# Attention on all four 64x64 tiles of TensorE, with the mask added in four half-size operations

## The chip, the core and the metric

The kernel runs on one core of a Trainium2 chip. Its engines work side by side and meet at semaphores: TensorE (PE; weight loads are shown as PEld), VectorE (DVE), ScalarE (ACT), GpSimd (POOL) and SyncE (SP), which starts DMAs. The metric is the device time of one execution in microseconds; less is better.

TensorE's array of 128 x 128 cells can be addressed in quarters, tiles of 64 x 64. The row half is given by the partitions on which the two inputs lie in SBUF, the column half by the partitions of PSUM that the output goes to. A float32 matmul stands in the trace as two records, each with its own weight load.

## What is computed

The reference is a small tower over 32 sequences of 64 tokens with 1024 features: a diagonal state-space filter, a rotary attention with 16 heads, a dequantized linear layer, a Mamba block and a linear layer with routed low-rank experts, each added to the residual. The change is in the attention:

```
q, k = rotary(x @ Wq), rotary(x @ Wk);  v = x @ Wv        # 16 heads of 64
logits = einsum('bhqd,bhkd->bhqk', q, k)
logits = where(causal, logits, -1e9) / sqrt(64)
attn = softmax(logits)
out = einsum('bhqk,bhkd->bhqd', attn, v)
h = h + out @ Wo
```

All of it is in float32; large products are split into a high and a low part in a rounded float32 form.

## The kernel before

The tokens are worked through in 4 blocks of 8 sequences (NB = 8, S = 64, so T = 512 tokens per block). Each block goes through all layers before the next one starts. Each weight matrix comes as strips of 128 output features: DMA brings a strip (`raw`), ScalarE makes its high part (`wh`), GpSimd the rest (`wl`, line 537), and TensorE runs 24 matmuls over it (`strip`, line 985). The order of all work is written out by hand, one program per engine, with semaphores between them.

Attention takes the 16 heads in 8 pairs (KC = 8), the one head on partitions 0 to 63, the other on 64 to 127. Per pair j TensorE runs three strips (q, k, v), and between them, for the pair of the step before, the transposes of the probabilities (`turned`, line 1093) and the weighted products (`weighted`, line 1105); behind the three strips come `logits` (line 1120) and the transposes of v (`values`, line 1129), which wait for VectorE's scaling of v (semaphore s_vT, line 1735). VectorE does the rotary sums, adds the mask (line 1686), takes the softmax (lines 1689 to 1695) and copies the outcome out of PSUM (line 1716); ScalarE does the exponential and the copies of v (`vf`) and of the transposed probabilities (`pT`).

In `logits` there are 16 small matmuls, for each sequence bb one of either head e: the head sets the row half and the column half alike, and the PSUM bank 2 + e. So head 0 is always computed in the tile (row half 0, column half 0) and head 1 in (1, 1). After it, `sm` has a head on each half of its partitions, all queries of a sequence in 64 columns.

The 16 transposed probability tiles lie in `pT` with the even sequences on partitions 0 to 63 and the odd ones on 64 to 127, side by side in the columns for the two halves of `sm`. In `weighted`, before, the eight matmuls of the even sequences come first (row half 0, column half e), then the eight of the odd ones (row half 1), into the banks 2 and 3.

Of the kernel before, what the change touches and what calls it, by code (L numbers as in the profile page):

```python
# [18 lines left out]
ALU = mybir.AluOpType  # L19
# [3 lines left out]
P = 128  # L23
# [3 lines left out]
NB = 8  # L27
# [155 lines left out]
def tower(nc, ins, out, nblk=NBLK, stop=9):  # L183
    with ExitStack() as ctx:
# [743 lines left out]
        def _(pe):  # L928
# [155 lines left out]
            for b in range(nblk):  # L1084
                if stop >= 2:
# [11 lines left out]
                    def weighted(j):  # L1097

                        pe.wait_ge(s_ptc, b * KC + j)
                        settle(pe)  # L1100
                        for par in range(2):
                            for bb in range(par, NB, 2):
                                for e in range(2):
                                    r0 = 64 * par
                                    ins_ = mm(psx[64 * e:64 * e + 64, 2 + par, bb * S:(bb + 1) * S],
                                              vf[r0:r0 + 64, (bb // 2) * P + 64 * e:(bb // 2) * P + 64 * e + 64],
                                              pT[r0:r0 + 64, (bb // 2) * P + 64 * e:(bb // 2) * P + 64 * e + 64],
                                              start=True, stop=True)
                        ins_.then_inc(s_pv, 1)

                    def logits(j):

                        pe.wait_ge(s_rot, b * 16 + 2 * j + 2)
                        if j >= 1:
                            pe.wait_ge(s_ao, b * KC + j)
                        settle(pe)
                        for bb in range(NB):
                            for e in range(2):
                                r0 = 64 * e
                                ins_ = mm(psx[r0:r0 + 64, 2 + e, bb * S:(bb + 1) * S],  # L1120
                                          qc[r0:r0 + 64, bb * S:(bb + 1) * S], kc[r0:r0 + 64, bb * S:(bb + 1) * S],
                                          start=True, stop=True)
                        ins_.then_inc(s_logit, 1)
# [301 lines left out]
        def _(v):  # L1425
# [249 lines left out]
            for b in range(nblk):  # L1675
                if stop >= 2:
                    norm(b, 0)
                    for j in range(KC + 1):
                        if j >= 1:
                            own = Own(v, s_own["soft"], b * 4 * KC + 4 * (j - 1))  # L1680
                            v.wait_ge(s_logit, b * KC + j)
                            if j >= 2:
                                v.wait_ge(s_ptm, b * KC + j - 1)
                            for e in range(2):
                                r = slice(64 * e, 64 * e + 64)
                                ins_ = tt(sm[r, :, :], psx[r, 2 + e, :].rearrange("p (b s) -> p b s", b=NB),
                                          over_b("causal", 64 * e, 64 * e + 64), ALU.add)
                            own.link(ins_)
                            own.link(v.tensor_reduce(smx[:, 0, :], sm[:, :, :], AXX, ALU.max))
                            tt(sm[:, :, :], sm[:, :, :], smx[:, 0, :].unsqueeze(2).to_broadcast([P, NB, S]),  # L1690
                               ALU.subtract).then_inc(s_ein, 1)
                            v.wait_ge(s_exp, b * KC + j)
                            own.link(v.tensor_reduce(smx[:, 1, :], sm[:, :, :], AXX, ALU.add))
                            own.link(v.reciprocal(smx[:, 1, :], smx[:, 1, :]))
                            tt(sm[:, :, :], sm[:, :, :], smx[:, 1, :].unsqueeze(2).to_broadcast([P, NB, S]),
                               ALU.mult).then_inc(s_prob, 1)
# [284 lines left out]
```

## Time and profile before

| | us |
|---|---|
| median of 3 runs | 4029.22 |
| lowest, highest | 4028.99, 4029.43 |
| profiled execution | 4035.27 |
| its span, first to last instruction | 4033.5 |
| TensorE matmuls busy | 3869.3 (96%) |
| VectorE busy | 2690.4 (67%) |
| GpSimd busy | 2212.4 (55%) |
| ScalarE busy | 2057.1 (51%) |
| granted clock of TensorE, mean | 0.984 of full |

The profile is one execution. Busy time is the time in which at least one instruction of the engine was under way; since matmuls overlap in the array, many records can be in flight at once, and their ends are modelled. "x" with a number is a count of records. Weight loads (PEld) overlap the matmuls. An arrow in brackets behind a row gives the idle time of the engine just before it, and who ended it; "issue" stands for no releaser that the profile shows.

### The profile page before, as it was taken

What the parts mean: (1) busy time and instruction counts of PE and PEld (TensorE: products, weight loads), DVE (VectorE), ACT (ScalarE), POOL (GpSimd) and SP (SyncE); (2) the same over time, 40 slices, a digit from 0 to 9 for tenths busy, and PEclk for the clock granted to TensorE, in tenths of its full rate; (3) what the DMA queues carried; (4) which work ended last, traced back from release to release, by engine and by line L of the source; (5) the groups of instructions that cost most, each with busy time, mean ns of one, the idle gap of its engine ahead of it and who ended that gap; (6) DMA issues with size and microseconds to landing.
All of it is one profiled execution on the core that took longest, in us unless ns stands there. A gap on an engine that the chain in (4) does not pass through costs nothing.

```text
span 4033.5 us, 59248 instructions
## 1 busy us (share of the span) xinstructions
PE 3869.3 (96%) x22816; PEld 2547.3 (63%) x22816; DVE 2690.4 (67%) x2934; ACT 2057.1 (51%) x3012; POOL 2212.4 (55%) x960
## 2 busy tenths in 40 slices
PE   4899999999999999999999999999999999999999
PEld 1568777444777777544577877744477877744466
DVE  6855572999446573699835555499935557289953
ACT  7842344777332344777523233677723234387732
POOL 0023433999534343799733334599943343389962
PEclk7999999999999999999999999999999999999999
DMA  4242234000322224200132223400032223410022
GB/s 114 79 145 80 86 104 159 23 16 16 118 93 86 79 84 137 98 16 16 61 114 95 79 77 117 153 13 16 26 125 94 84 84 105 160 31 16 16 89 73
DMA packets 97131, 320.23 MB, mean 79 GB/s; under 512 B 12400, under 2 KB 16752, under 8 KB 92400
## 3 DMA queue, kind: packets, MB, share of 16 engines
q1 hardware_dynamic: 80752, 275.70, 21.4%
q10 hardware_dynamic: 16128, 41.03, 3.0%
q8 instruction: 176, 2.88, 0.3%
q14 instruction: 75, 0.61, 0.1%
HBM read 272.51 MB, written 44.17 MB: 79 GB/s over the span
## 4 chain that ended last, share of the span: by engine, by line
PE 36%; issue 32%; DVE 20%; POOL 9%; ACT 2%; POOLq 0%; ACTq 0%; DVEq 0%
PE psg L985 22%; DVE sb_wst L1798 17%; POOL sb_wl L537 9%; PE psx L1220 5%; PE psg L1241 3%; PE psx L1293 1%; PE psg L1271 1%; DVE psg L1771 1%; DVE psg L1770 1%; PE psg L1369 1%; PE psg L1278 1%; ACT sb_yh L898 1%; PE psx L1002 0%; PE psg L1260 0%; PE psg L1195 0%
## 5 line engine op out<-in xcount | busy, mean ns | idle before, releaser
L537 POOL TENSOR_TENSOR sb_wl<-sb_raw,sb_wh 128x1024 fp32r<-128x1024 f32 x388 | 955.1, 2465 | 1740.9 <-ACT sb_wh L654 1740.6
L1798 DVE TENSOR_TENSOR_SCAN sb_wst<-sb_dA,psx 128x1024 f32<-128x1024 f32 x512 | 1130.0, 2268 | 12.3 <-PE psx L1220 10.4
L654 ACT ACTIVATE sb_wh<-sb_raw 128x1024 fp32r<-128x1024 f32 x388 | 407.4, 1053 | 544.1 <-PE psg L985 268.8
L796 ACT ACTIVATE sb_dA<-sb_dlt,sb_a_sb 128x504 f32<-128x504 f32 x1024 | 647.3, 705 | 56.0 <-DVE sb_wst L1798 53.8
L1220 PEld LDWEIGHTS psx<-sb_dgB,sb_duT 64*128 64x128 f32 x4096 | 359.9, 188 | 447.5 <-DVE sb_wst L1798 309.1
L1220 PE MATMUL psx<-sb_dgB,sb_duT 64*128 64x256 f32 x4096 | 587.5, 406 | 35.3 <-DVE sb_wst L1798 33.3
L1241 PE MATMUL psg<-sb_wst,sb_cst 64*64 64x512 f32 x4096 | 605.7, 617 | 0.9 <-ACT sb_twin L787 0.9
L572 POOL TENSOR_TENSOR sb_wst<-sb_wst,sb_cb_lo 128x1024 f32<-128x1024 f32 x256 | 600.3, 2370 | 5.0 <-DVE sb_wst L1798 5.0
L572 POOL TENSOR_TENSOR sb_wst<-sb_wst,sb_cb_hi 128x1024 f32<-128x1024 f32 x248 | 577.6, 2365 | 24.7 <-DVE sb_wst L1798 24.7
L985 PE MATMUL psg<-sb_xh,sb_wh 128*128 128x512 f32 x2080 | 535.6, 400 | 16.1 <-POOL sb_wl L537 7.1
L985 PE MATMUL psg<-sb_xh,sb_wl 128*128 128x512 f32 x2080 | 516.7, 390 | 0.0
L985 PE MATMUL psg<-sb_xl,sb_wh 128*128 128x512 f32 x2080 | 513.9, 389 | 0.0
L985 PEld LDWEIGHTS psg<-sb_xh,sb_wh 128*128 128x128 f32 x2080 | 384.0, 189 | 112.8 <-issue 15.3
L985 PEld LDWEIGHTS psg<-sb_xh,sb_wl 128*128 128x128 f32 x2080 | 391.2, 188 | 83.2
L985 PEld LDWEIGHTS psg<-sb_xl,sb_wh 128*128 128x128 f32 x2080 | 390.4, 188 | 81.3
L1241 PEld LDWEIGHTS psg<-sb_wst,sb_cst 64*64 64x64 f32 x4096 | 123.3, 132 | 186.2 <-issue 186.1
L1824 DVE TENSOR_TENSOR psg<-psg,sb_rstd 128x512 f32<-128x512 f32 x60 | 42.0, 699 | 286.0 <-PE psg L985 286.0
L1876 DVE TENSOR_TENSOR sb_h<-sb_h,psg 128x512 f32<-128x512 f32 x32 | 22.0, 687 | 257.1 <-PE psg L985 222.9
L1760 DVE SCALAR_TENSOR_TENSOR sb_cv<-psg,sb_conv,sb_cv 128x504 f32<-128x504 f32 (+2 forms) x192 | 141.0, 734 | 27.8 <-DVE sb_cv L1758 4.1
L787 ACT ACTIVATE sb_twin<-psg 128x512 f32<-128x512 f32 x128 | 69.3, 593 | 118.6 <-PE psg L1249 118.6
L705 ACT ACTIVATE sb_ah<-sb_ao 128x512 fp32r<-128x512 f32 x32 | 20.2, 632 | 193.2 <-DVE sb_ao L1716 193.2
L662 ACT ACTIVATE sb_xh<-sb_xc 128x512 fp32r<-128x512 f32 x128 | 79.2, 618 | 76.6 <-DVE sb_xc L1599 66.6
(278 smaller groups left out, 4946.9 us busy)
## 6 DMA issues: line engine op xcount, KB each, us to landing
sb_raw<-in_w SPq DMA_DIRECT2D x360, 512.0 KB, 3.6
sb_raw<-w_ffn_dequantized SPq DMA_DIRECT2D x32, 512.0 KB, 3.3
gates<-sb_gt ACTq DMA_DIRECT2D x64, 256.0 KB, 2.6
sb_gin<-gates SPq DMA_DIRECT2D x64, 256.0 KB, 2.6
h_after_tok<-sb_h SPq DMA_DIRECT2D x4, 2048.0 KB, 8.7
sb_cb_lo<-c_rows ACTq DMA_DIRECT2D x8, 1024.0 KB, 6.2
sb_cb_hi<-c_rows ACTq DMA_DIRECT2D x8, 1024.0 KB, 7.5
sb_h<-h_after_tok SPq DMA_DIRECT2D x4, 2048.0 KB, 8.5
```

The costliest lines, as they stand in the source:

```text
L537: pool.tensor_tensor(rest(b, i0), raw[:, i0 % RAW, :, :], high(b, i0).bitcast(F32), ALU.subtract).then_inc(s_wl, 1)
L572: pool.tensor_tensor(x, x, cb, ALU.mult).then_inc(s_p, 1)
L654: A(high(b, i0), raw[:, i0 % RAW, :, :], ACT.Copy).then_inc(s_wh, 1)
L662: A(xh[:, k, :], xc[:, k, :], ACT.Copy).then_inc(s_xh, 1)
L787: ins_ = A(twin[:, r, :], psg[:, r, :], ACT.Copy)
L796: ins_ = A(dA[:, (m * NQ + k) % RING, :, n, 1:S], dlt[:, m % 2, :].rearrange("p (b s) -> p b s", b=NB)[:, :, 1:S], ACT.Exp, scale=a_sb[:, ...
L985: ins_ = mm(psg[:, bank, :], w_[:, s_, k, :], x_[:, k0 + k, :], start=start and n == 0, stop=stop_ and n == 3 * KC - 1)
L1220: ins_ = mm(psx[:, 2 * j + r, :].rearrange("p (a t e) -> p a t e", a=8, e=2)[:, :, :, e], duT[r0:r0 + 64, m % 2, i * P:(i + 1) * P], dgB[r ...
L1241: ins_ = mm(psg[64 * c:64 * c + 64, r, :], C("fold")[r0:r0 + 64, :], wst[r0:r0 + 64, (m * NQ + k) % RING, :, 2 * half + c, :], start=(k == ...
L1760: ins_ = stt(y[:, :, d:S], x[:, :, 0:S - d], tap(3 - d), y[:, :, d:S], ALU.mult, ALU.add)
L1798: v.tensor_tensor_scan(wst[:, x, 4 * j:4 * j + 4, :, :].rearrange("p b n s -> p (b n s)"), dA[:, x, 4 * j:4 * j + 4, :, :].rearrange("p b ...
L1824: tt(psg[:, m % 2, :], psg[:, m % 2, :], rstd[:, :], ALU.mult).then_inc(s_gr, 1)
```

## The change

In `logits`, the column half now is `e ^ bb % 2`: for even sequences it is the head, as before, for odd ones the other half. The bank stays 2 + e. Four matmuls in a row (two sequences, two heads) so go to four different tiles. In `sm`, the odd sequences have their heads on exchanged halves of the partitions.

In `weighted`, the sequences come in their own order, so that the row half (bb % 2) alternates after every two matmuls; the columns of `pT` that are read follow the exchange (`c0`), and what is written, where, and by how many matmuls stays.

The addition of the mask reads, for either half of the partitions, the even sequences from one bank and the odd ones from the other: four operations on 64 x 4 x 64 elements, where two on 64 x 512 were.

```diff
                         pe.wait_ge(s_ptc, b * KC + j)
                         settle(pe)
-                        for par in range(2):
-                            for bb in range(par, NB, 2):
-                                for e in range(2):
-                                    r0 = 64 * par
-                                    ins_ = mm(psx[64 * e:64 * e + 64, 2 + par, bb * S:(bb + 1) * S],
-                                              vf[r0:r0 + 64, (bb // 2) * P + 64 * e:(bb // 2) * P + 64 * e + 64],
-                                              pT[r0:r0 + 64, (bb // 2) * P + 64 * e:(bb // 2) * P + 64 * e + 64],
-                                              start=True, stop=True)
+                        for bb in range(NB):
+                            for e in range(2):
+                                r0, c0 = 64 * (bb % 2), 64 * (e ^ bb % 2)
+                                ins_ = mm(psx[64 * e:64 * e + 64, 2 + bb % 2, bb * S:(bb + 1) * S],
+                                          vf[r0:r0 + 64, (bb // 2) * P + 64 * e:(bb // 2) * P + 64 * e + 64],
+                                          pT[r0:r0 + 64, (bb // 2) * P + c0:(bb // 2) * P + c0 + 64],
+                                          start=True, stop=True)
                         ins_.then_inc(s_pv, 1)
...
                         for bb in range(NB):
                             for e in range(2):
-                                r0 = 64 * e
-                                ins_ = mm(psx[r0:r0 + 64, 2 + e, bb * S:(bb + 1) * S],
+                                r0, c0 = 64 * e, 64 * (e ^ bb % 2)
+                                ins_ = mm(psx[c0:c0 + 64, 2 + e, bb * S:(bb + 1) * S],
                                           qc[r0:r0 + 64, bb * S:(bb + 1) * S], kc[r0:r0 + 64, bb * S:(bb + 1) * S],
                                           start=True, stop=True)
                         ins_.then_inc(s_logit, 1)
...
-                            for e in range(2):
-                                r = slice(64 * e, 64 * e + 64)
-                                ins_ = tt(sm[r, :, :], psx[r, 2 + e, :].rearrange("p (b s) -> p b s", b=NB),
-                                          over_b("causal", 64 * e, 64 * e + 64), ALU.add)
+                            for c in range(2):
+                                for par in range(2):
+                                    r = slice(64 * c, 64 * c + 64)
+                                    ins_ = tt(sm[r, :, :].rearrange("p (a t) s -> p t a s", t=2)[:, par, :, :],
+                                              psx[r, 2 + (c ^ par), :].rearrange("p (a t s) -> p t a s", t=2, s=S)[:, par, :, :],
+                                              C("causal")[r, :].unsqueeze(1).to_broadcast([64, NB // 2, S]), ALU.add)
                             own.link(ins_)
```

On VectorE, this is the place of the mask's addition in the second pair of the first block, before; `sb_vT` is the scaled v, `s_logit` the end of the logits.

```order
L1735 TENSOR_TENSOR sb_vT<-psg,sb_rstd 128x512 [waits s_vtm,s_strip]
L1686 TENSOR_TENSOR sb_sm<-psx,sb_cst 64x512 [waits s_ptm,s_logit]
L1686 TENSOR_TENSOR sb_sm<-psx,sb_cst 64x512
L1689 TENSOR_REDUCE sb_smx<-sb_sm 128x8 [waits s_own_soft]
L1690 TENSOR_TENSOR sb_sm<-sb_sm,sb_smx 128x512 [waits s_own_soft]
```

The same place of the changed kernel, whose lines below the edit bear other numbers:

```order
L1736 TENSOR_TENSOR sb_vT<-psg,sb_rstd 128x512 [waits s_vtm,s_strip]
L1686 TENSOR_TENSOR sb_sm<-psx,sb_cst 64x4x64 [waits s_ptm,s_logit]
L1686 TENSOR_TENSOR sb_sm<-psx,sb_cst 64x4x64 x3
L1690 TENSOR_REDUCE sb_smx<-sb_sm 128x8 [waits s_own_soft]
L1691 TENSOR_TENSOR sb_sm<-sb_sm,sb_smx 128x512 [waits s_own_soft]
```

Two additions became four of half the size; what waits for what is as it was.

On TensorE, the queue around the logits of the changed kernel, which is that of the kernel before save for the line numbers (1119 was 1120, 1128 was 1129), since the change exchanges matmuls within the groups of 16 alone:

```order
L985 MATMUL psg<-sb_xl,sb_wh 128x512 x8
L1119 MATMUL psx<-sb_kc,sb_qc 64x64 [waits s_rot,s_ao]
L1119 MATMUL psx<-sb_kc,sb_qc 64x64 x15
L1128 MATMUL psg<-sb_cst,sb_vT 128x128 [waits s_vT]
L1128 MATMUL psg<-sb_cst,sb_vT 128x128 x3
```

No instruction moved past another group; the transposes of v, which wait for s_vT, stand right behind the logits as before.

## Rows read from the trace of the kernel before

**Rows 1.** Page: busy times; forty slices, TensorE and its granted clock in tenths.

```profile
PE 3869.3 (96%) x22816; PEld 2547.3 (63%) x22816; DVE 2690.4 (67%) x2934; ACT 2057.1 (51%) x3012; POOL 2212.4 (55%) x960
...
PE   4899999999999999999999999999999999999999
...
PEclk7999999999999999999999999999999999999999
```

**Rows 2.** Windows over the four attention stretches: length, busy us, clock, DMA.

```profile
core 0: us, PE busy (x) PEld busy (x) DVE busy (x) ACT busy (x) POOL busy (x), PEclk, DMA share, GB/s
273.00:422.00 149.00, 149.00 (x1117) 121.04 (x1117) 87.08 (x160) 41.63 (x55) 56.50 (x23) 1.00 0.25 78
...
3108.00:3257.00 149.00, 149.00 (x1117) 121.04 (x1116) 87.10 (x160) 41.63 (x55) 56.53 (x23) 1.00 0.24 77
```

**Rows 3.** Timeline of TensorE over one period: start, us, line, tiles, count.

```profile
1271.37 1.15 PE L1120 MATMUL psx<-sb_kc,sb_qc 64*64 64x64 f32 x32
1272.45 0.66 PE L1129 MATMUL psg<-sb_cst,sb_vT 128*128 128x128 f32 x4
...
1278.43 0.60 PE L1093 MATMUL psg<-sb_cst,sb_sm 128*128 128x128 f32 x4
...
1284.45 0.98 PE L1105 MATMUL psx<-sb_pT,sb_vf 64*64 64x64 f32 x32
...
1291.03 1.15 PE L1120 MATMUL psx<-sb_kc,sb_qc 64*64 64x64 f32 x32
```

**Rows 4.** Lines 1120 and 1105: durations in ns, least, median, most; count.

```profile
L1120 PE MATMUL psx<-sb_kc,sb_qc x1024: 218/218/268, 273.8 to 3241.9; 64*64 64x64 f32 x171
...
L1105 PE MATMUL psx<-sb_pT,sb_vf x1024: 218/218/267, 284.2 to 3251.6; 64*64 64x64 f32 x171
```

**Rows 5.** Windows of 0.12 us: TensorE's records in flight (x); logits, then weighted.

```profile
core 0: us, PE busy (x), PEclk, DMA share, GB/s
1271.60:1271.72 0.12, 0.12 (x11) 1.00 0.00 0
1271.84:1271.96 0.12, 0.12 (x12) 1.00 0.00 0
1284.60:1284.72 0.12, 0.12 (x8) 1.00 0.00 0
1284.84:1284.96 0.12, 0.12 (x16) 1.00 0.09 34
```

**Rows 6.** Timeline of TensorE in the scan stage: two tiles, then four.

```profile
802.42 1.13 PE L1220 MATMUL psx<-sb_dgB,sb_duT 64*128 64x256 f32 x8
803.48 1.09 PE L1241 MATMUL psg<-sb_wst,sb_cst 64*64 64x512 f32 x8
```

**Rows 7.** Timeline behind one logits group, VectorE (DVE) and weight loads (PEld).

```profile
1271.48 0.69 DVE L1735 TENSOR_TENSOR sb_vT<-psg,sb_rstd 128x512 f32<-128x512 f32 x1 [1.63 <-PE psg L985]
...
1272.45 0.42 PEld L1129 LDWEIGHTS psg<-sb_cst,sb_vT 128*128 128x128 f32 x4
...
1272.57 1.39 DVE L1686 TENSOR_TENSOR sb_sm<-psx,sb_cst 64x512 f32<-64x512 f32 x2 [0.40 <-PE psx L1120]
...
1274.00 0.69 DVE L1689 TENSOR_REDUCE sb_smx<-sb_sm 128x8 f32<-128x512 f32 x1
...
1277.07 0.69 DVE L1695 TENSOR_TENSOR sb_sm<-sb_sm,sb_smx 128x512 f32<-128x512 f32 x1
...
1278.20 0.59 PEld L1093 LDWEIGHTS psg<-sb_cst,sb_sm 128*128 128x128 f32 x4
```

**Rows 8.** Timelines: a scan of VectorE, and TensorE's load that it releases.

```profile
854.82 2.29 DVE L1798 TENSOR_TENSOR_SCAN sb_wst<-sb_dA,psx 128x1024 f32<-128x1024 f32 x1
...
857.16 0.19 PEld L1220 LDWEIGHTS psx<-sb_dgB,sb_duT 64*128 64x128 f32 x2 [0.86 <-DVE sb_wst L1798]
```

**Rows 9.** Timeline of VectorE behind the first logits of a block.

```profile
275.01 1.39 DVE L1686 TENSOR_TENSOR sb_sm<-psx,sb_cst 64x512 f32<-64x512 f32 x2 [5.09 <-PE psx L1120]
```

**Rows 10.** Timeline of VectorE: the two half-size copies out of banks 2, 3.

```profile
1286.97 0.75 DVE L1716 COPY sb_ao<-psx 128x256 f32<-128x256 f32 x2
```

## The prediction

> **What bounds the kernel now.** I read the slices of the page first: TensorE is busy 96% of the span, and from the second slice on nine tenths or more at a clock of 0.9 and above, that is 2.4 GHz [rows 1]. The change lies in the attention stage, so the windows over its four passes come next. In each of the four stretches of 149.00 us TensorE is busy 149.00 us, at clock 1.00, while VectorE is busy 87 us, ScalarE 42 us and GpSimd 57 us [rows 2]. The list of waits has not one wait of TensorE's matmuls there. What TensorE saves in this stage is saved in the kernel, unless another engine becomes late.
>
> The timeline of one period shows how it is spent [rows 3]: from one logits group (1271.37) to the next (1291.03) 19.66 us, of which the logits show 1.15 us, the transposes of v 0.66, the transposes of the probabilities 0.60 and the weighted products 0.98; the rest is three weight strips. There are 32 logits groups and 32 weighted groups (4 blocks x 8 head pairs), 1024 matmul records of each [rows 4]. The two groups have the same 32 records of the same shape (a float32 matmul shows as two records), and yet one takes 0.17 us longer. The reader should see why, since it prices the change.
>
> **How fast two tiles go, and four.** A matmul record lasts 0.218 us, but they overlap [rows 4]. The logits' first start and last start are 1.15 - 0.22 = 0.93 us apart. Their two tiles hand in a pair of records every 0.93/16 = 0.058 us. The old weighted group does all eight of its matmuls on row half 0, then eight on row half 1. Counting the records in flight in stretches of 0.12 us [rows 5]: two stretches of the logits hold 11 and 12; of the weighted group the first (still filling) 8, and the one in its middle, where the second row half starts while the first is still running, 16. There TensorE runs four tiles at once: (16 - 0.22/0.03) is about 8 new records in 0.12 us, four per 0.06, against two per 0.058 in the logits. That overlap is some three rounds long, and 3 x 0.058 = 0.17 us is just what the weighted group is shorter. Four tiles at full rate are seen elsewhere too: eight 64x64 records of 512 columns (two rounds of four tiles) take 1.09 us, eight 64x128 records of 256 columns (four rounds of two) 1.13 us [rows 6].
>
> **The change, part by part.**
>
> Logits: 32 records in 8 rounds of four instead of 16 rounds of two. The first round is dearer than the rest in both (it fills the array), so I take a little under half off: 0.93 - 0.455 = 0.475 us from first to last start, 0.455 us less.
>
> Weighted products: before, 0.98 - 0.22 = 0.76 us from first to last start [rows 3, 4]; after, the same 8 rounds of four as the logits, 0.475. That is 0.28 us less. Behind them stands a strip whose weights were ready long before, so all of it counts: 32 x 0.28 = 9.0 us.
>
> What is late next behind the logits: TensorE's transposes of v, which wait for VectorE's scaling of v (line 1735). That scaling starts when the strip before the logits ends, beside the logits, and runs 1271.48 + 0.69 = 1272.17 [rows 7]. TensorE's load released by VectorE starts 0.05 us behind its end: scan 854.82 + 2.29 = 857.11, load at 857.16 [rows 8]. So the transposes' load can't start before 1272.22. Before the change it started at 1272.45 [rows 7]; without the scaling it would now start at 1272.45 - 0.455 = 1272.00. So of 0.455 us only 1272.45 - 1272.22 = 0.23 us is kept, and TensorE stands still for the rest. In the first pair of each block it is otherwise: another strip stands between v's strip and the logits, and VectorE idles 5.09 us before the mask addition [rows 9], so v is long scaled and the whole 0.455 is kept. Sum: 28 x 0.23 + 4 x 0.455 = 6.4 + 1.8 = 8.2 us.
>
> The mask's addition: two operations on 64x512 (1.39 us together, and 1.43 from the first start to the next operation [rows 7]) become four on 64x256. The trace of before has no addition of that size. Nearest is the copy out of the same two banks, 128x256: two of them in 0.75 us, so 0.41 us each with 0.33 between starts [rows 10]. Lower bound: starts 0.33 apart save where the partition half changes, 0.33 + 0.42 + 0.33 + 0.42 = 1.50 us, 0.11 more than now. Upper bound from that row: none overlaps, 4 x 0.42 = 1.7 us, 0.3 more. A gain is excluded, since the same 1024 elements per partition lane are passed over and two more starts come on top. I take 0.14, as the copies lie in the same banks with the same stride.
>
> It costs nothing as long as the probabilities come before TensorE wants them. Now VectorE's last softmax step ends at 1277.07 + 0.69 = 1277.76, plus 0.05 is 1277.81; the load of the probability transposes starts at 1278.20 [rows 7]: 0.39 us of cover. After the change TensorE comes there 0.23 us earlier, the addition starts at about 1272.12 instead of 1272.57 (0.45 earlier: the logits end that much earlier, and v's scaling is just over) and takes 0.14 longer. Cover: 0.39 - 0.23 + 0.45 - 0.14 = 0.47 us; with the upper price 0.3 us. For the first pair of a block 0.39 - 0.455 + 0.455 - 0.14 = 0.25, or 0.1 at the upper price. If the cover were gone, each 0.1 us of lateness would cost 28 x 0.1 = 2.8 us.
>
> No DMA, weight strip or wait is added or moved. GpSimd's four splits (7.7 us busy by the four-stretch row: 57 of 149) follow TensorE's pace, and a stage 0.4% faster asks nothing new of them.
>
> **Sum.** 9.0 + 8.2 = 17.2 us. The profiled execution took 4035.3 us (span 4033.5); the changed one should take 4018.1. Against the median of 4029.2 this makes 4012.0 us.
>
> **Two rules weighed.** The weighted group's first half keeps both its tiles in row half 0, and the group is shorter than the logits', not longer [rows 3, 4]: two column tiles of one row half get in each other's way nowhere in it. The Trainium skill ("TensorE: Matmul & The Clock Gate", The mechanism) says that a weight load overlaps running matmuls only where the row group differs. By that rule each row half, which now serves two column tiles in turn, would come out as in rival (c); this case's trace speaks against it.
>
> The mean gap between starts is 0.93/31 = 0.030 us in the logits and 0.76/31 = 0.025 in the weighted group, with two tiles running for most of either [rows 3, 4]; where four run it is about 0.015 [rows 5]. The same page (Back-to-back issue gap) puts a floor of about 25 ns under a matmul of up to 64 columns. Were it a floor over all tiles together, the outcome would lie near rival (a), some 4 us gained; the stretch with four tiles lies below it.
>
> **Rivals.**
>
> (a) Four tiles only in a short spell: the overlap seen is three rounds long, and records queued beforehand may have fed it. If TensorE can't issue faster over a whole group than the weighted group's mean, the logits come down to 0.76 and the weighted group stays: 32 x 0.17 = 5.4 us, 4023.8 us. Against it: rounds of four with 512 columns, though these need fewer issues per us. A milder form, rounds of 0.075 or 0.088 us instead of 0.058, gives group lengths of 0.58 or 0.66: saved 28 x 0.23 + 4 x 0.35 + 32 x 0.175 = 13.4 (4015.8) or 28 x 0.23 + 4 x 0.27 + 32 x 0.095 = 10.6 us (4018.6).
>
> (b) The scaling of v doesn't hold the transposes, the whole 0.455 is kept in all 32: 14.6 + 9.0 = 23.6 us, 4005.6 us. Against it: the order of waits, s_vT on the transposes' first matmul.
>
> (c) Slower, by tiles of one row half: each record must wait for its own load. Row half 0 has 16 records per group; at 0.058 for the stream and as much for the load a group lasts 16 x 0.116 = 1.86 us from first to last, 0.93 and 1.1 more: 32 x 2.0 = 65 us, 4094 us. It decides from 0.116 us per round on, where the logits gain nothing. Against it: the weighted group's first half.
>
> (d) Slower, by the mask's addition: a half-size operation costs as much as a full one. Then 4 x 0.70 = 2.8 us, 1.4 more than now, cover 0.39 - 0.23 + 0.45 - 1.4 = -0.8 us per pair, against 0.51 saved: 28 x 0.8 = 22 us lost of 17 gained, 4034 us. It decides from about 0.57 us per operation, against the 0.41 of the copies.
>
> (e) The gain is taken back elsewhere, by a wait later in the block that doesn't move with TensorE: 4029 us. Against it: the regular 19.66 us and no wait in the stage.
>
> **Chances and range.** Forecast (4009 to 4015): 0.76. Milder form of (a), 4015 to 4019: 0.05. (a) 0.07, (b) 0.04, (c) 0.01, (d) 0.02, (e) 0.05. The range from 4005 to 4019 holds the first two and (b). About 0.2% (8 us) is what a measurement of this kernel tells from no change, so faster begins below 4021: faster 0.85; same, which takes (a) and (e), 0.12; slower 0.03.
>
> **What the changed profile would show.** Logits and weighted groups of about 0.70 us each instead of 1.15 and 0.98; some 23 records in flight in 0.12 us (0.22 x 4/0.058 + 8); the load of v's transposes 0.05 us behind the end of VectorE's scaling, in 28 of 32; a period of 19.66 - 0.51 = 19.15 us; four mask additions in 1.5 us. The load of the probability transposes still in the middle of a running strip. A group longer than 0.75 us proves (a), a gap of TensorE before the probability transposes (d), a period of 18.93 us (b), and a period of 19.15 with an unchanged total (e).

## The result and the profile after

The change makes the kernel faster by more than was predicted, and the time falls below the predicted range.

| | before, us | after, us |
|---|---|---|
| median (6 runs each) | 4029.32 | 4004.29 |
| lowest, highest | 4028.16, 4031.62 (and one of 12831, an outlier) | 3999.10, 4007.14 |
| ratio, 95% interval | | 0.9936 (0.9923 to 0.9950) |
| profiled execution; its span | 4035.27; 4033.5 | 4007.14; 4005.3 |
| granted clock of TensorE, mean | 0.984 | 0.988 |

The gain is 25.0 us; 17.2 were forecast, 4012.0 with a range of 4005 to 4019.

What was forecast of the attention stage came within some hundredths of a microsecond per period. The timeline of TensorE over one period of the changed kernel, against [rows 3] (start, length, line, tiles, count):

```profile
1261.89 0.69 PE L1119 MATMUL psx<-sb_kc,sb_qc 64*64 64x64 f32 x32
1262.75 0.66 PE L1128 MATMUL psg<-sb_cst,sb_vT 128*128 128x128 f32 x4 [0.16 <-DVE sb_vT L1736]
...
1268.74 0.60 PE L1093 MATMUL psg<-sb_cst,sb_sm 128*128 128x128 f32 x4
...
1274.76 0.69 PE L1104 MATMUL psx<-sb_pT,sb_vf 64*64 64x64 f32 x32
...
1281.06 0.69 PE L1119 MATMUL psx<-sb_kc,sb_qc 64*64 64x64 f32 x32
```

Logits and weighted groups both last 0.69 us, where they took 1.15 and 0.98; 0.70 was forecast. The period is 1281.06 - 1261.89 = 19.17 us; 19.15 was forecast. Records in flight in 0.12 us of a logits group, against [rows 5] (TensorE's busy time, in brackets the records):

```profile
1262.08:1262.20 0.12, 0.12 (x20) 1.00 0.00 0
1262.20:1262.32 0.12, 0.12 (x24) 1.00 0.00 0
```

24 against the 11 and 12 of before (23 were forecast), each record as long as ever (218 ns, the median of line 1119 as of line 1120 in [rows 4]). The same place seen from VectorE and the weight loads, against [rows 7]:

```profile
1262.00 0.69 DVE L1736 TENSOR_TENSOR sb_vT<-psg,sb_rstd 128x512 f32<-128x512 f32 x1 [1.33 <-PE psg L985]
1262.66 1.53 DVE L1686 TENSOR_TENSOR sb_sm<-psx,sb_cst 64x256 f32<-64x256 f32 x4
1262.75 0.42 PEld L1128 LDWEIGHTS psg<-sb_cst,sb_vT 128*128 128x128 f32 x4 [0.30 <-DVE sb_vT L1736]
...
1267.29 0.69 DVE L1696 TENSOR_TENSOR sb_sm<-sb_sm,sb_smx 128x512 f32<-128x512 f32 x1
...
1268.51 0.59 PEld L1093 LDWEIGHTS psg<-sb_cst,sb_sm 128*128 128x128 f32 x4
```

The scaling of v ends at 1262.00 + 0.69 = 1262.69, and the load of v's transposes starts at 1262.75: here the trace names VectorE as what TensorE waited for, where the trace of before had no such wait. The addition follows the scaling at once and takes 1.53 us (1.50 to 1.7 was the range, 1.39 the time before). The last softmax step ends at 1267.98, the load that needs it starts at 1268.51: 0.53 us, 0.05 of them the signal's way, so 0.48 of cover; 0.47 was forecast.

From the first logits matmul of a block to its last weighted one an attention pass took 142.84 us before, in each of the four blocks, and takes 138.55 to 138.59 now: 17.1 us less in all. So the other 8 us of the gain lie outside the attention, where nothing was changed. The granted clock differs there. Windows of 8 us in the blocks 2 and 3 before, around the first matmuls behind a layer's norm (1450, 2396) and around the start of the scan (1656, 2601), columns as in [rows 2]:

```profile
1450.00:1458.00 8.00, 6.40 (x22) 4.25 (x24) 7.29 (x13) 6.57 (x13) 0.00 (x0) 0.79 0.00 0
1656.00:1664.00 8.00, 6.85 (x32) 3.13 (x30) 8.00 (x4) 6.27 (x9) 8.00 (x5) 0.59 0.07 29
2396.00:2404.00 8.00, 6.40 (x25) 4.22 (x24) 7.71 (x13) 6.99 (x14) 0.00 (x0) 0.79 0.01 3
2601.00:2609.00 8.00, 6.55 (x32) 3.36 (x32) 8.00 (x5) 6.27 (x10) 8.00 (x4) 0.62 0.01 3
```

The same four places of the changed kernel:

```profile
1438.00:1446.00 8.00, 6.40 (x29) 3.41 (x28) 7.29 (x13) 6.57 (x13) 0.00 (x0) 1.00 0.00 0
```

```profile
1642.00:1650.00 8.00, 5.26 (x40) 3.00 (x40) 8.00 (x5) 6.26 (x10) 8.00 (x4) 1.00 0.00 0
```

```profile
2376.50:2384.50 8.00, 6.40 (x29) 3.62 (x29) 7.57 (x13) 6.85 (x14) 0.00 (x0) 1.00 0.01 2
```

```profile
2580.50:2588.50 8.00, 5.69 (x32) 2.87 (x32) 8.00 (x5) 6.26 (x9) 8.00 (x4) 0.79 0.01 6
```

Before, the clock was at its lower level, 1.2 GHz, for a part of each; after, three of the four are at 2.4 GHz throughout. What TensorE did ahead of the first of these places is the same in both: behind the sums of a norm it stands still for 1.60 us, then strips start. What follows differs (timeline of TensorE, before and after):

```profile
1452.21 0.47 PE L1023 MATMUL psg<-sb_xh,sb_wh 128*128 128x512 f32 x1 [1.60 <-ACT sb_xh L662]
...
1453.24 0.63 PE L1023 MATMUL psg<-sb_xh,sb_wl 128*128 128x512 f32 x1
1453.67 0.63 PE L1023 MATMUL psg<-sb_xh,sb_wh 128*128 128x512 f32 x1
1454.10 0.63 PE L1023 MATMUL psg<-sb_xh,sb_wl 128*128 128x512 f32 x1
```

```profile
1440.20 0.47 PE L1023 MATMUL psg<-sb_xh,sb_wh 128*128 128x512 f32 x1 [1.60 <-ACT sb_xh L662]
...
1440.73 0.39 PE L1023 MATMUL psg<-sb_xh,sb_wh 128*128 128x512 f32 x1
1440.96 0.40 PE L1023 MATMUL psg<-sb_xh,sb_wl 128*128 128x512 f32 x1
```

0.43 us from record to record against 0.23: for the eight records or so that fall under this dip of the clock the matmuls take almost twice as long.

From here on "the rest" is the time from the end of the first attention pass to the end, less the three other passes; "under the lower clock" is how long in it the records show the lower level. I add both up from the starts in each trace. Before: 3188.3 us, 44 under the lower clock. After: 3181.8 us, 17 under it. The part ahead of the first attention, in the kernels alike, took 273.8 and 269.3 us. So the two profiled executions differ by 28.1 us (4.5 ahead, 17.1 in the attention, 6.5 in the rest), the medians by 25.0.

The two traces can be laid side by side, since outside the attention both run the same code: I cut the rest at the same instructions into stretches of some 8 us and compare their lengths. The stretches that have the lower clock in neither trace, nor within 3 us of them, are 2998 of the 3188 us; in sum they differ by 0.01 us. The whole difference of 6.5 us lies in the other 191 us, at the dips.

### The profile page after: what moved, and what is told of

The parts are those of the page before. It is cut to its first block, busy times and chain, and to the rows that moved or that the text cites. A ratio compares the mean times of both kernels' runs of the same rounds, so it can differ in the third digit from the quotient of the medians.

```text
span 4005.3 us, 59312 instructions
## 1 busy us (share of the span) xinstructions
PE 3834.2 (96%) x22816; PEld 2514.5 (63%) x22816; DVE 2696.4 (67%) x2998; ACT 2056.8 (51%) x3012; POOL 2212.5 (55%) x960
## 3 DMA queue, kind: packets, MB, share of 16 engines
q1 hardware_dynamic: 80752, 275.70, 21.6%
## 4 chain that ended last, share of the span: by engine, by line
PE 36%; issue 32%; DVE 20%; POOL 9%; ACT 2%; POOLq 0%; ACTq 0%; DVEq 0%
PE psg L985 22%; DVE sb_wst L1799 17%; POOL sb_wl L537 9%; PE psx L1219 5%; PE psg L1240 3%; PE psx L1292 1%; PE psg L1270 1%; DVE psg L1772 1%; DVE psg L1771 1%; PE psg L1368 1%; PE psg L1277 1%; ACT sb_yh L898 1%; PE psx L1002 0%; PE psg L1259 0%; PE psg L1194 0%
## 5 line engine op out<-in xcount | busy, mean ns | idle before, releaser
L1825 DVE TENSOR_TENSOR psg<-psg,sb_rstd 128x512 f32<-128x512 f32 x60 | 42.0, 700 | 286.0 <-PE psg L985 286.0
L1629 DVE TENSOR_TENSOR psg<-psg,sb_rstd 128x512 f32<-128x512 f32 x64 | 44.5, 695 | 110.0 <-PE psg L1390 75.4
```

What stands on the lines that cost most here:

```text
L1629: Own(v, s_own["scale"], b * SCALES + at).link(tt(x, x, rstd[:, :], ALU.mult))
```

## The experiments

Two theories stood against each other. Theory 1: the gain beyond the sum comes from the clock alone; shifting the work moves it out of the places where the clock dips. Theory 2: it belongs to an edit, most likely to the four-tile groups. All kernels of a set were compared with runs of the kernel before on the same chip; its medians in the three sets were 4029.04, 4030.67 and 4029.97 us (60 runs from 4019.7 to 4035.8).

### The parts one at a time

`e1_logits`: the change, the weighted products in their old order.

```diff
-                        for bb in range(NB):
+                        for bb in [*range(0, NB, 2), *range(1, NB, 2)]:
                             for e in range(2):
                                 r0, c0 = 64 * (bb % 2), 64 * (e ^ bb % 2)
```

> The logits and the mask as in the change; the weighted products in the old order (even sequences first, then odd), with the columns of pT that the exchanged halves need. The computation is the whole one. Both theories: logits 0.477 us from first to last start, transposes of v 0.377 behind it in 28 of 32, weighted 0.757: 28 x 0.226 + 4 x 0.453 = 8.1 us less in the attention stage, period 19.43 us. Theory 1 (the 8 us that the change gained beyond its sum come from the granted clock outside the attention, whose dips fall elsewhere or nowhere once the work is shifted, and belong to no edit): the time outside the attention differs from before by some us, and only where the granted clock differs; the total 4021 with 8 us to either side at the most, 4013 to 4023. Theory 2 (the 8 us belong to the four-tile groups, since fuller use of the array changes what follows): outside the attention some 4 us less, 4017, the same in each run.

Measured: 4015.70 us, 13.3 less than before, ratio 0.9964 (0.9952 to 0.9977). The attention is 7.8 us shorter. Weighted is back at its old length, logits is as in the change:

```profile
1260.51 0.69 PE L1119 MATMUL psx<-sb_kc,sb_qc 64*64 64x64 f32 x32
1261.37 0.65 PE L1128 MATMUL psg<-sb_cst,sb_vT 128*128 128x128 f32 x4 [0.16 <-DVE sb_vT L1736]
...
1273.38 0.98 PE L1104 MATMUL psx<-sb_pT,sb_vf 64*64 64x64 f32 x32
```

`e2_weighted`: the kernel before, the weighted products in the new order alone.

```diff
-                        for par in range(2):
-                            for bb in range(par, NB, 2):
-                                for e in range(2):
-                                    r0 = 64 * par
+                        for bb in range(NB):
+                            for e in range(2):
+                                r0, c0 = 64 * (bb % 2), 64 * e
```

> Only the order of the weighted products is changed; logits and mask as before. The computation is the whole one. Both theories: weighted 0.477 instead of 0.757 us from first to last start, 32 x 0.28 = 9.0 us less in the attention stage, period 19.38 us. Theory 1 (granted clock outside the attention, by shift of the work): total 4020 with the outside part wandering by some us with the clock, 4012 to 4022. Theory 2 (belongs to the four-tile groups): outside the attention some 4 us less, 4016, the same in each run.

Measured: 4018.36 us, 10.7 less, ratio 0.9966 (0.9952 to 0.9980). The attention is 9.3 us shorter.

`e3_mask`: the kernel before, the addition in four operations alone.

```diff
-                            for e in range(2):
-                                r = slice(64 * e, 64 * e + 64)
-                                ins_ = tt(sm[r, :, :], psx[r, 2 + e, :].rearrange("p (b s) -> p b s", b=NB),
-                                          over_b("causal", 64 * e, 64 * e + 64), ALU.add)
+                            for c in range(2):
+                                for par in range(2):
+                                    r = slice(64 * c, 64 * c + 64)
+                                    ins_ = tt(sm[r, :, :].rearrange("p (a t) s -> p t a s", t=2)[:, par, :, :],
+                                              psx[r, 2 + c, :].rearrange("p (a t s) -> p t a s", t=2, s=S)[:, par, :, :],
+                                              C("causal")[r, :].unsqueeze(1).to_broadcast([64, NB // 2, S]), ALU.add)
```

> Only the mask's addition is changed to four half-size operations; the matmuls are those of before. The computation is the whole one. The addition takes 1.53 instead of 1.39 us, and the load of the probability transposes still starts in the middle of a strip: period 19.66 us, no change in the attention. Both theories: 4029 within 1 us, since nothing on TensorE is shifted and the clock's dips stay where they are. Rival (d) of the prediction: above 4031.

Measured: 4027.97 us, ratio 0.9998 (0.9988 to 1.0007), attention passes of 142.82 to 142.84 us. The addition takes 1.53 us and costs nothing:

```profile
1272.15 1.53 DVE L1687 TENSOR_TENSOR sb_sm<-psx,sb_cst 64x256 f32<-64x256 f32 x4 [0.40 <-PE psx L1120]
```

In its trace the rest is 3188.2 us with 44 under the lower clock: the numbers of before, from another execution. Its dips in the rest stand where before's do, within 0.1 us behind the end of a block's attention pass. That was the first hint that, where no work is shifted, they can come back to the same places.

The attention parts add up (7.8 + 9.3 = 17.1), and so do the totals (13.3 + 10.7 = 24.0 of 25.0). Theory 2 could still be right with the logits as the owner: their kernel has 5.5 us too much, that of the weighted products 1.4.

### Shifting the work without the edit, and the edit without the shift

`e7_padded`: four tiles, but groups as long as before.

```diff
                         # weighted
-                        for bb in range(NB):
+                        for bb in [*range(NB), *range(5)]:
...
                         # logits
-                        for bb in range(NB):
+                        for bb in [*range(NB)] * 2:
```

> The change with padding: every logits group issues its 16 matmuls twice, every weighted group its first ten again (26 in all), over the same outcomes, so that four tiles run but either group lasts as long as before (0.944 and 0.755 us from first to last start against 0.930 and 0.757). The work is the whole one and some of it twice. Both theories: attention passes of 142.9 us, as before. Theory 1 (the gain beyond the sum comes from where the clock's dips fall outside the attention, which follows from the timing alone): with the timing of before, the total of before, 4029.5, between 4027 and 4032, passes between attentions of 801 to 803 us. Theory 2 (the gain beyond the sum, 5 to 8 us in all runs with the new logits, comes with the four-tile groups, wherever they end): outside the attention 5 to 8 us less than before, total 4022 to 4024.

Measured: 4030.47 us against 4030.67, ratio 1.0000 (0.9991 to 1.0009). The weighted groups came out at 0.813 instead of 0.755 us from first to last start (a round more than I had worked out), so that the passes are 143.26 us long, 1.7 us more in all than before. With four tiles in every group, only 1.9 us are left over beyond what the attention explains, where theory 2 wanted 4022 to 4024. (In its trace, one execution, the rest is 4.3 us shorter than before's, with 25 us under the lower clock instead of 44.)

`e6_before_longer` and `e8_before_longer2`: the kernel before, two tiles at a time, the first logits group of each block three and five times.

```diff
-                        for bb in range(NB):
+                        for bb in [*range(NB)] * (3 if j == 0 else 1):
```

> The kernel before, with the first logits group of each block issued three times over the same outcomes: 2 x 16 x 0.0583 = 1.87 us more per block in the attention, 7.5 us in all; no four-tile groups. The work is the whole one and some of it twice. Without any effect of timing on the clock: 4029.2 + 7.5 = 4036.7. Theory 1 (a shift of the work alone changes how much of the time outside falls under the lower clock): off that by some us, most likely below it, 4029 to 4036, with granted clock above 0.984. Theory 2 (the extra gain needs four-tile groups): 4036.7 within 1.5 us.

> As the run before it, with the first logits group of each block issued five times: 3.73 us more per block, 14.9 in all; no four-tile groups. Without any effect of timing on the clock: 4044.1. Theory 1: off that by some us, most likely below, 4036 to 4043. Theory 2: 4044.1 within 1.5 us.

Measured: 4033.88 us, 3.2 more than before where 7.5 us of work were added, ratio 1.0006 (0.9997 to 1.0015); and 4043.53, 12.9 more where 14.9 were added, ratio 1.0036 (1.0023 to 1.0050). The passes are longer by 1.87 and 3.73 us each, as they should. The kernel with more work gets 4.3 us back outside the attention, without one group on four tiles; in its trace the rest is 3181.1 us with 13 under the lower clock. Two of the places that dipped before (columns as in [rows 2]):

```profile
1442.00:1462.00 20.00, 17.68 (x76) 10.61 (x75) 12.63 (x19) 9.75 (x19) 0.95 (x1) 1.00 0.09 27
...
2380.00:2425.00 45.00, 41.43 (x179) 30.02 (x178) 33.19 (x44) 19.63 (x29) 11.97 (x5) 1.00 0.18 57
```

Theory 2 falls with it: four tiles are not needed for a gain outside the attention. The second kernel is weaker evidence: 2.0 us off, barely more than the 1.5 that theory 2 allowed.

`e10_before_once`: the same repeat (five times), in the first block alone.

```diff
-                        for bb in range(NB):
+                        for bb in [*range(NB)] * (5 if j == 0 and b == 0 else 1):
```

> The kernel before, with the first logits group of the first block alone issued five times: 3.73 us more, once; blocks of the same length as before after it. If the length of a block is what matters: before's time plus 3.7, 4033.5 within 1.5 us. If the place of the stages behind the kernel's start matters, off that by some us.

Measured: 4035.17 us, 5.2 more than before where 3.7 were added, ratio 1.0015 (1.0007 to 1.0024). In its trace the rest is 3188.4 us with 44 under the lower clock, as in the kernel before and in `e3_mask`, though from the second block on all of it starts 3.3 us nearer to the kernel's begin. The three kernels whose later blocks have before's length have the same rest, within 0.2 us, and the same places of the dips. That points to the length of a block, and not to where the stages begin; but it is one execution of each kernel, and the only shifts tried are 0.4 us (`e3_mask`) and 3.3.

The trace gives besides the size of what varies from run to run. Up to the first logits this kernel's code is that of before, and yet it is there after 266.82 us, against 273.82 before:

```profile
266.82 2.37 PE L1120 MATMUL psx<-sb_kc,sb_qc 64*64 64x64 f32 x74
```

75 us of it are under the lower clock, 82 before. In that first stage TensorE has pauses (four tenths busy in the first slice of [rows 1]), and where its dips fall differs from execution to execution. Over the traces it takes from 266.8 to 273.8 us. The profiled execution of before, at 4035.3, has the longest of the fourteen.

`e11_after_same_period`: the change with the first logits group of each block ten times.

```diff
-                        for bb in range(NB):
+                        for bb in [*range(NB)] * (10 if j == 0 else 1):
                             for e in range(2):
                                 r0, c0 = 64 * e, 64 * (e ^ bb % 2)
```

> The changed kernel with the first logits group of each block issued ten times over the same outcomes: 9 x 8 rounds x 0.0583 = 4.2 us more per block, so that each attention pass is as long as before (142.8), though by one pad at its head. The work is the whole one and some of it twice. By the sum alone: the change plus 16.8 us, 4021 from the change's 4004.3. If the extra gain of the change hangs on the length of a block (with before's length all four blocks meet the clock's dips at the same places): back to before's 4029.5 within 2 us. If neither, but it is kept: 4021.

Measured: 4034.34 us, ratio 1.0013 (1.0005 to 1.0022). It doesn't tell what it was made to tell, since the blocks did not get before's length: the pad took 5.5 to 7.7 us per block instead of 4.2, and the attention 578.5 us, 7.2 more than before. The reason is a finding of its own (last section). Against before it has 2.8 us less than its added work; the rest is 3185.3 us with 34 under the lower clock, between before and the others.

### The wait that the change brought, and the order in the queue

`e4_values_later`, timed again as `e12_values_later_again`: the transposes of v of the pairs 1 to 6 behind the first two matmuls of the next strip.

```diff
-                            strip(b, 3 * j, 0, 0, xh, xl)
+                            strip(b, 3 * j, 0, 0, xh, xl, between=lambda: values(j - 1), at=2)
...
                         logits(j)
-                        values(j)
+                        if j == KC - 1:
+                            values(j)
```

> The change, and besides the transposes of v of the pairs 1 to 6 issued after the first two matmuls of the next strip instead of right behind the logits. The computation is the whole one. If VectorE's scaling of v is what holds TensorE for 0.23 us behind the logits, the strip starts 0.15 us behind the last logits matmul and the stall is gone in 24 of 28 places: 24 x 0.226 = 5.4 us less than the change in the attention, period 18.93 us for the pairs concerned. If the gap is a drain between tile sizes, not a wait, it stays 0.377 in front of the strip and the period 19.16. Theory 1: total 4012.0 - 5.4 = 4006.6 by the sum, less up to 10 us by the clock; theory 2: 4004.3 - 5.4 = 3998.9.

> The change with the transposes of v of the pairs 1 to 6 behind the first two matmuls of the next strip, timed again beside the change itself. The attention passes are 4 x 1.1 = 4.5 us shorter than the change's. If that carries through: 4.5 us below the change in this set. If the clock's dips outside the attention give it back by the other timing, as the first runs had it (4003.0 against 4004.3): 1 to 2 us below.

Measured: 4003.00 us, ratio 0.9931 (0.9915 to 0.9948), and 4003.79, ratio 0.9936 (0.9922 to 0.9949). The stall is gone; strip and transposes follow without a gap:

```profile
1217.73 0.69 PE L1119 MATMUL psx<-sb_kc,sb_qc 64*64 64x64 f32 x32
1218.35 0.73 PE L985 MATMUL psg<-sb_xh,sb_wh 128*128 128x512 f32 x2
1218.92 0.60 PE L1128 MATMUL psg<-sb_cst,sb_vT 128*128 128x128 f32 x4
1219.28 0.94 PE L985 MATMUL psg<-sb_xh,sb_wh 128*128 128x512 f32 x3
```

The strip's first record starts 0.62 us behind the group's, the old 0.855 held the stall. So it was VectorE's scaling, not a drain. The passes are 137.43 us, 4.5 us less than the change in all (0.19 per place, where 0.226 were expected; where the difference goes I did not look into). The total fell by 1.3 us only: in both traces 21 to 28 us of the rest are under the lower clock, against 17 and 12 in the change's two. That is the way in which 3.2 us would be given back; with six runs spread over 11 us in the second set, how much was is not settled. It is the fastest kernel of the study by its median, but not by more than the measurement can tell from the change.

`e5_grouped`: the change, with the logits of the even sequences first, then the odd.

```diff
-                        for bb in range(NB):
+                        for bb in [*range(0, NB, 2), *range(1, NB, 2)]:
                             for e in range(2):
                                 r0, c0 = 64 * e, 64 * (e ^ bb % 2)
```

> The change, but with the 16 logits matmuls in another order: the even sequences' eight first (tiles (0,0) and (1,1)), then the odd ones' eight (the other two tiles). Same matmuls, same tiles, whole computation. If what counts is that neighbours in the queue go to four tiles, the group runs at two tiles with one crossover, as the old weighted group, 0.757 us from first to last start instead of 0.477; or without any crossover, as both row halves are held by the first half, 0.93. The transposes of v then start 0.149 behind: 0.906 or 1.08 behind the group's start, against 0.855 in the change, so 28 x 0.05 + 4 x 0.28 = 2.5 us or 28 x 0.225 + 4 x 0.45 = 8.1 us more than the change in the attention. If the mapping to tiles alone counts, there is no difference.

Measured: 4008.18 us, ratio 0.9946 (0.9930 to 0.9961); attention 2.8 us longer than the change's (2.5 was expected), the total 3.1 to 3.9.

```profile
1261.26 0.98 PE L1119 MATMUL psx<-sb_kc,sb_qc 64*64 64x64 f32 x32
1262.17 0.66 PE L1128 MATMUL psg<-sb_cst,sb_vT 128*128 128x128 f32 x4
```

0.98 us, the length of the old weighted group: the same 16 matmuls on the same tiles give less when neighbours in the queue use two tiles, with a short crossover in the middle. This is the reading of [rows 5] put to the test from the other side.

`e9_after_again`: the changed kernel, timed once more.

> The changed kernel as it is, timed in more rounds beside the others of this set. If the 25 us measured first are what the change gives, 4003 to 4006. If a lucky draw of the clock's dips was part of them, the median moves up towards the sum's 4012.

Measured: 4005.08 us (4003.73 to 4006.58), ratio 0.9942 (0.9929 to 0.9954), 24.9 us less than before. The rest is 3179.1 us with 12 under the lower clock. So the 25 us are no lucky draw.

### All of them side by side

"Difference" is the median against that of before in the same set; "attention" is what the four passes of the trace explain of it; "left over" what remains.

| kernel | difference | attention | left over | rest in the trace | under the lower clock |
|---|---|---|---|---|---|
| before | 0 | 0 | 0 | 3188.3 | 44 |
| e3_mask | -1.1 | 0.0 | -1.1 | 3188.2 | 44 |
| e10_before_once | +5.2 | +3.7 | +1.5 | 3188.4 | 44 |
| e8_before_longer2 | +12.9 | +14.9 | -2.0 | 3187.3 | 35 |
| e11_after_same_period | +4.4 | +7.2 | -2.8 | 3185.3 | 34 |
| e2_weighted | -10.7 | -9.3 | -1.4 | 3184.0 | 28 |
| e7_padded | -0.2 | +1.7 | -1.9 | 3184.0 | 25 |
| e5_grouped | -22.5 | -14.3 | -8.2 | 3183.5 | 28 |
| e12_values_later_again | -26.2 | -21.6 | -4.6 | 3183.1 | 21 |
| e4_values_later | -26.0 | -21.7 | -4.3 | 3182.8 | 28 |
| e1_logits | -13.3 | -7.8 | -5.5 | 3182.8 | 28 |
| after | -25.0 | -17.1 | -7.9 | 3181.8 | 17 |
| e6_before_longer | +3.2 | +7.5 | -4.3 | 3181.1 | 13 |
| e9_after_again | -24.9 | -17.0 | -7.9 | 3179.1 | 12 |

The rest goes with the time under the lower clock: 9.2 us between 44 and 12, about 0.3 us for each. The left-over medians go the same way, with a scatter of one or two us (four to twelve runs each, and the draw of the first stage on top). In each of the other twelve traces, too, laid beside that of before, the stretches away from the dips agree within 0.4 us in sum.

The mean clock is on record for every run, not only for the profiled ones, and twice what it lacks, times the span, is the time under the lower level. Averaged over a kernel's runs and set against the runs of before in the same set, that time is 27 us less in `e9_after_again`, 21 and 22 in `e6_before_longer` and `e5_grouped`, 10 to 17 in the runs `e1`, `e2`, `e4`, `e7`, `e8`, `e11` and `e12`, 2 less in `e3_mask` and 3 more in `e10_before_once`: nearly the order of the left-over column. The same record limits what the three traces with 44 us say. The 60 runs of before have clocks of 0.983 to 0.989, an estimate of 137 to 88 us under the lower level. The first stage held 72 to 89 us of it in the traces, so the run at 0.989, 4019.7 us long, had at most some 20 left for the rest. Before's length does not bring 44 in every execution.

## Why the prediction was wrong

**The bound, and four tiles in turn: right.** TensorE bounds the stage, and its savings came through. The rate of four tiles, read off a short overlap of the old weighted group, held over whole groups: 0.69 us each. Rival (a) and its milder form are refuted for groups of this size.

**The wait that takes the saving's place: right.** 0.23 us of 0.455 kept behind the logits in 28 of 32, VectorE named as the releaser; `e4_values_later` removed it. Rival (b) is out.

**The mask's addition: right.** 1.53 us, and no effect (`e3_mask`); rival (d) is out. Rival (c) is out too: in the change each row half serves two column tiles in turn, 24 records are in flight, and the groups are shorter, not longer. The Trainium skill ("TensorE: Matmul & The Clock Gate", The mechanism) says that weight loads overlap running matmuls only in another row group; this case does not bear that out. The 32 records of a group start within 0.69 - 0.22 = 0.47 us, 15 ns apart. The floor of about 25 ns from start to start that the Trainium skill ("TensorE: Matmul & The Clock Gate", Back-to-back issue gap) gives for up to 64 columns is not one over all tiles together.

**The step that failed** is the first one, "what TensorE saves in this stage is saved in the kernel". The sum of 17.2 us was taken over to the total one for one, as if the rest of the kernel would be the same, only earlier. Measured are 17.1 us in the attention and 8 more outside it: the failing term is the change outside the attention, which the sum put at nothing without a reason. Rival (e) did look at the rest, but as a place where a gain could be lost to a wait; that it could gain, through the clock, was no case of mine, and so no part of the range reached below 4005. The number that would have warned me was read and not used: the mean clock of 0.984 over the span. The slices could not, and I read them wrongly: a 9 stands for anything from 0.90 up, so it does not say 2.4 GHz throughout. At half speed for a share x the mean is 1 - x/2, so 1.6% of missing clock is 3.2% of the span, about 129 us, under the lower level (127 by the records); a change that shifts work can win or lose a part of what that costs, to either side. The three runs that I had, 0.4 us from lowest to highest, made it look steady; later sets of the same kernel spread over 16 us.

**A slip that changed nothing.** The prediction calls the stage 0.4% faster where it asks about GpSimd. That is the share of the kernel; the attention pass became 3.0% shorter (142.84 to 138.55). GpSimd kept up all the same, since the passes came out as forecast.

**What stays open.** Shown is that what the rest gains or loses lies at the dips of the clock, and that a shift of work without the edit moves it too (`e6_before_longer`). That it is the length of a block that counts, and not the distance from the start, rests on three traces and is likely rather than shown. Why before's block length in particular meets the dips in every block of these traces is not shown, nor what sets the place of a dip. That before's length is an unlucky one among many is an inference from fourteen traces, and two other lengths (`e8_before_longer2`, `e11_after_same_period`) come near it.

## What to carry to other kernels

Small matmuls on quarters of the array should go to all four tiles in turn in the order of the queue; the same matmuls grouped by tile give only a part of it. Before counting the gain, look at which operation on another engine starts with the group and how long it lasts: here it took half of the gain behind the logits, and moving two matmuls ahead of the waiting transposes took the stall away, though of its 4.5 us only 1.3 were seen in the total. Where the mean clock of the page is below one, carry a term for it in the range on both sides: here it was 8 us on a sum of 17, and from one profiled execution to another the first stage alone varied by 7.0 us.

## What the hardware showed that was not expected

A long run on four tiles stopped on the way. In `e11_after_same_period` 320 records stand in a row on four tiles (timeline of TensorE, then its weight loads in windows of 1 us):

```profile
270.29 4.19 PE L1119 MATMUL psx<-sb_kc,sb_qc 64*64 64x64 f32 x270
275.52 0.97 PE L1119 MATMUL psx<-sb_kc,sb_qc 64*64 64x64 f32 x50 [1.05 <-issue]
```

```profile
270.50:271.50 1.00, 1.00 (x76) 1.00 0.91 221
...
273.00:274.00 1.00, 1.00 (x76) 1.00 0.07 16
274.00:275.00 1.00, 0.34 (x23) 1.00 0.00 0
```

After 270 records, started within 4.19 - 0.22 = 3.97 us, TensorE stands still for 1.05 us without a releaser that the profile shows, and then goes on. In the other three blocks it stops after 223, 176 (and again after 304) and 257 records; from block to block the group took 6.0 to 8.1 us from first to last start, where 80 rounds of 0.058 make 4.7. Two tiles at a time kept their rate over 160 records in a row (4.664 us, in `e8_before_longer2`). The cause is open: that instructions are used up faster than they arrive would be one, and no run tests it. It is what rival (a) feared, at a length that the kernel's groups of 32 records don't reach.
